# Products that nobody reads on TensorE, in a decoder of four layers: at the seams between stages and in front of waits inside them

## The reference

```python
x = _layernorm(x + _L0_attn_ref(x, L0_attn_W_in, ...), axis=-1)
x = _layernorm(x + _L0_xattn_ref(x, ctx_768, L0_xattn_Wq, ...), axis=-1)
x = _layernorm(x + _L0_ffn_ref(x, L0_ffn_gate_w, ...), axis=-1)
...
x = _layernorm(x + _L3_ffn_ref(x, L3_ffn_ln_scale, ...), axis=-1)
```

```python
# layer 1, feed-forward
logits = xf @ Wr                                  # 8 columns
top_vals, top_idx = jax.lax.top_k(logits, TOP_K)
...
h = _sq_relu(jnp.einsum('td,edf->tef', xf, W1))
# layer 2, feed-forward
d2 = x2 + p2[None, :] - 2.0 * (xf @ prototypes.T) # 32 columns
w = jax.nn.softmax(-jnp.sqrt(jnp.maximum(d2, 0.0)) / t, axis=1)
topw, topi = jax.lax.top_k(w, 2)
```

## Time and profile before

| what | value |
| --- | --- |
| timed runs | 3248.4, 3252.83 and 3253.66 us |
| median | 3252.83 us |
| span of the profiled execution, first to last instruction | 3262.6 us |
| a time of its own for the profiled execution, beside the span | none given |
| PE busy | 2508.7 us (77%), 15890 products |
| DVE, ACT, POOL busy | 57%, 45%, 31% |
| granted TensorE clock, mean of the span | 0.879 |
| DMA, mean | 53 GB/s |

### The profile page before, as it was taken

The page is one execution under the profiler, slowest core; times in us unless marked ns, Lnnn a source line. Parts: engine busy times, 40 slices in busy tenths (PEclk is TensorE's granted clock), DMA queues, the critical chain, the costliest instruction groups (busy, mean ns, idle before and its releaser), DMA issues. The chain is left out here.

```text
span 3262.6 us, 45065 instructions
## 1 busy us (share of the span) xinstructions
PE 2508.7 (77%) x15890; PEld 1399.0 (43%) x15890; DVE 1855.3 (57%) x5014; ACT 1480.5 (45%) x2984; POOL 996.1 (31%) x822
## 2 busy tenths in 40 slices
PE   6788885785667577888874669897776788859977
PEld 2323324564443233333352255564443333346666
DVE  6576655565645455555553558335432577656678
ACT  5334451453432156666641514224412355537876
POOL 1145561146347566666612300001101111101200
PEclk9889998897878789999986869997687799978989
DMA  3311101610444411111002210001000322114023
GB/s 112 94 43 42 42 2 36 229 54 19 125 154 101 108 47 46 35 41 46 17 15 67 34 39 1 10 4 30 14 1 33 74 28 28 16 48 123 1 78 104
DMA packets 186942, 174.52 MB, mean 53 GB/s; under 512 B 52777, under 2 KB 160042, under 8 KB 186462
## 3 DMA queue, kind: packets, MB, share of 16 engines
q1 hardware_dynamic: 172030, 153.84, 16.8%
q0 software_dynamic: 9408, 12.56, 2.5%
q10 hardware_dynamic: 5280, 5.24, 0.5%
HBM read 117.62 MB, written 57.40 MB: 54 GB/s over the span
## 5 line engine op out<-in xcount | busy, mean ns | idle before, releaser
L946 POOL TENSOR_TENSOR l1a_p_lo<-res,l1a_p_hi 128x1024 f16<-128x1024 f32 x192 | 311.9, 1643 | 177.2 <-ACT res L1187 177.2
L1196 ACT ACTIVATE l0a_probs<-ps 128x1024 f32<-128x1024 f32 (+1 forms) x192 | 145.5, 810 | 176.2 <-PE ps L1050 103.7
L1196 ACT ACTIVATE l3a_probs<-ps 128x1024 f32<-128x1024 f32 (+1 forms) x192 | 146.9, 809 | 143.3 <-PE ps L1050 116.2
L1186 ACT ACTIVATE l1a_p_hi<-ps 128x1024 f16<-128x1024 f32 x192 | 157.8, 822 | 110.9 <-PE ps L1050 82.8
L1047 PE MATMUL ps<-l1a_qs,l1a_ks 128*128 128x512 f16 (+3 forms) x768 | 167.7, 333 | 31.6 <-ACT res L1187 31.6
L1016 PE MATMUL ps<-l1a_ks,l1a_qs 128*128 128x512 f16 (+3 forms) x384 | 122.2, 347 | 78.7 <-DVE l1a_nmax L1221 33.0
L1218 DVE CUSTOM_DVE_ANT_0 l1a_masked<-ps,l1a_wide_mask 128x128 bf16<-128x128 f32 (+3 forms) x256 | 118.0, 490 | 103.1 <-PE ps L1016 100.9
L971 POOL TENSOR_TENSOR l0a_both<-l0a_probs 128x768 f32<-128x768 f32 (+2 forms) x96 | 154.7, 1633 | 46.3 <-PE ps L1088 46.0
L1187 ACT ACTIVATE res<-ps 128x1024 f32<-128x1024 f32 x192 | 158.1, 823 | 0.0
L1050 PE MATMUL ps<-mask_t,ident_b 128*128 128x128 bf16 x768 | 157.5, 225 | 0.0
L1218 DVE CUSTOM_DVE_ANT_0 l0a_masked<-ps,l0a_wide_mask 128x128 bf16<-128x128 f32 (+3 forms) x256 | 116.5, 489 | 68.0 <-PE ps L1016 67.3
(11 more groups left out here) (749 smaller groups left out, 6453.7 us busy)
## 6 DMA issues: line engine op xcount, KB each, us to landing
f_wf<-in_L_ffn_w_dram SPq DMA_DIRECT2D x16, 1024.0 KB
f_slots<-x0a_zeros SPq DMA_DIRECT2D x32, 256.0 KB, 3.4
f_xe<-f_slots SPq DMA_DIRECT2D x32, 256.0 KB, 3.0
f_ys<-f_y SPq DMA_DIRECT2D x32, 256.0 KB
l1a_qs<-l_q_h SPq DMA_DIRECT2D x64, 128.0 KB
d_wall<-in_L_ffn_W_dram SPq DMA_DIRECT2D x3, 2112.0 KB
l0a_qs<-l_q_h SPq DMA_DIRECT2D x32, 128.0 KB
l0a_ks<-l_k_h SPq DMA_DIRECT2D x16, 256.0 KB
```

The costliest lines, as they stand in the source:

```text
L946: pool.tensor_tensor(ph_lo[:, n % SLOTS, :, 0:w], probs[:, n % FULL, :, 0:w], ph_hi[:, n % SLOTS, :, 0:w], ALU.subtract).then_inc(s_["low_ ...
L1186: act.activation(ph_hi[:, n % SLOTS, :, 0:w], SB[n % 2][:, :, 0:w], ACT.Exp)
L1196: act.activation(probs[0:KR, n % SLOTS, 2 * pr:2 * pr + 2, 0:w], SB[x % 2][:, :, 0:w], ACT.Exp).then_inc(s_["exps"], 1)
```

## The change

A new function issues n products into a PSUM bank that the place does not use at that moment. Each multiplies the 128x128 16-bit identity with the identity repeated four times, 512 columns; nobody reads the result, and no semaphore is signalled by it. Calls of it are put at 112 places that issue 893 such products in the whole program. Where the place stands in front of a wait on data, a wait on the bank's last reader is moved ahead of it, or added.

```diff
+    def keep_busy(self, pe, bank, n):
+        for _ in range(n):
+            pe.matmul(bank, self.ident_b[:], self.ident_b[:, None, :].to_broadcast([P, 4, P]), start=True, stop=True)
...
 class Tail: __init__
+        self.busy = (0, 0)
 class Tail: tensor
+        after(pe, ph.s["xts_ready"], g)
+        if g == NG - 1:
+            ph.k.keep_busy(pe, self.tp[:, 0, :], self.busy[0])
         pe.wait_ge(ph.s["xn_ready"], g + 1)
-        after(pe, ph.s["xts_ready"], g)
         for c in range(DC):
...
         ins.then_inc(ph.s["xn_turned"], 1)
+        if g == NG - 1:
+            ph.k.keep_busy(pe, ph.k.ps[:, 2, :], self.busy[1])
 norm_program
-            pe.wait_ge(ph.s["n_xc_ready"], g + 1)
             if g >= NB:
                 pe.wait_ge(ph.s["n_ready"], g - NB + 1)
+            if within:
+                k.keep_busy(pe, TP[g % NB][:, 0, :], 9)
+            pe.wait_ge(ph.s["n_xc_ready"], g + 1)
 packed_attention, the row factor
                         pe.wait_ge(s_["maxed"], a - NSA + 1)
+                        if own_sums and plan.key_rows == P:
+                            k.keep_busy(pe, sa, 9)
                         pe.wait_ge(r_ld[s % KEEP], 32 * (s // KEEP + 1))
 packed_attention, scores
-                    if u.first and pr == 0:
-                        pe.wait_ge(m_ld[s % LEAD], 32 * (s // LEAD + 1))
...
+                    if plan.key_rows < P and n == 0 and pr == 0:
+                        k.keep_busy(pe, k.ps[:, 2, :], 18)
+                    if u.first and pr == 0:
+                        pe.wait_ge(m_ld[s % LEAD], 32 * (s // LEAD + 1))
 project_columns
+        tail.busy = (40 if pre else 20, 4)
+                k.keep_busy(pe, k.ps[:, 2, :], 16 if pre else 12)
                 pe.wait_ge(ph.s["w_ld"], n_ld)
 project_halves
+        tail.busy = (16, 4)
+                k.keep_busy(pe, k.ps[:, 2, :], 28)
 turn_out
+        tail.busy = (14, 4)
 project_out
+                tail.busy = (16, 4)
 l0_self_attention, for each batch b and c in range(EC)
+                            if b:
+                                pe.wait_ge(ph.s["v_ready"], b * TB)
+                            k.keep_busy(pe, PV[0], (0, 4, 4, 9)[c])
 project_in, busy=8
+            k.keep_busy(pe, k.ps[:, 0, :], busy)
 rotary_projection
+                if t % GT < 3:
+                    k.keep_busy(pe, k.ps[:, 5, :], 4)
             def columns(g):
+                if g:
+                    pe.wait_ge(s_["v_moved"], g)
+                k.keep_busy(pe, k.ps[:, 6, :], 11)
                 pe.wait_ge(s_["xn_ready"], g + 1)
...
                 ins.then_inc(s_["xn_turned"], 1)
+                k.keep_busy(pe, k.ps[:, 6, :], 8)
 l3_self_attention, stage l3e
+                    k.keep_busy(pe, k.ps[:, 0, :], 14)
 context, start and end
+                k.keep_busy(pe, bank[0], 20)
+                k.keep_busy(pe, k.ps[:, 4, :], 16)
 cross_operators, start and end
                 if columns is None:
+                    k.keep_busy(pe, bank[0], 16 if shared else 11)
                     turned_context(pe)
                 products(pe, done, NJ)
+                k.keep_busy(pe, k.ps[:, 6, :], 12)
 cross_rows, turn of batch a of tile t, x = NBT * t + a
-                    pe.wait_ge(s_["normed"], NH * t + needs[a])
                     if x >= 2:
                         pe.wait_ge(s_["lower"], x - 1)
+                    if x == 0:
+                        k.keep_busy(pe, TP[0], 14 if NH > 1 else 6)
+                    elif NH == 1:
+                        k.keep_busy(pe, TP[x % 2], 2)
+                    pe.wait_ge(s_["normed"], NH * t + needs[a])
 routed_experts, start
+                k.keep_busy(pe, k.ps[:, 0, :], 7)
 l1_feed_forward
+                k.keep_busy(pe, k.ps[:, 1, :], 4)
                 pe.wait_ge(s_["g_ld"], 16)
...
                 hidden(0)
+                k.keep_busy(pe, k.ps[:, 2, :], 24)
                 pe.wait_ge(s_["gates_ready"], 1)
...
+                k.keep_busy(pe, k.ps[:, 0, :], 18)
                 columns(NG - 1)
+                k.keep_busy(pe, k.ps[:, 0, :], 4)
 l2_feed_forward
                 def turn(t):
-                    pe.wait_ge(s_["weighted"], t + 1)
                     if t >= 2:
                         pe.wait_ge(s_["moved"], t - 1)
+                        k.keep_busy(pe, TP[t % 2], 4)
+                    pe.wait_ge(s_["weighted"], t + 1)
...
+                k.keep_busy(pe, k.ps[:, 4, :], 10)
                 pe.wait_ge(s_["p_ld"], 32)
...
                 lower(1)
+                k.keep_busy(pe, k.ps[:, 5, :], 16)
...
+                k.keep_busy(pe, k.ps[:, 0, :], 11)
                 columns(NG - 1, NT)
+                k.keep_busy(pe, k.ps[:, 0, :], 4)
```

More of the change, by code:

```diff
@@ L1824, in row_parts, with project_in @@
     return parts
-def project_in(k, ph, jobs, loads, split=False, early=None, apart=False):
+def project_in(k, ph, jobs, loads, split=False, early=None, apart=False, busy=8):
     nc = k.nc
```

## The result

The changed kernel took 3229.97 us at the median (3226.85 to 3238.05), the kernel before 3253.24 us; the ratio is 0.993, 95% interval [0.9913, 0.9947]. That is 23.3 us saved where 49.3 were forecast. The direction was right and the time lies inside the stated range, but the size is less than half.

What follows compares the result with a forecast made beforehand. PE was taken as busiest, its work after waits slowed by a low clock (24% of the span). Gains of 80.5 us less costs of 31.2 gave 49.3 us off the 3252.8 median: 3203 us, own range 3180 to 3222, outer 3160 to 3240.

Steps and rivals of the forecast that it cites:

- the sum inside stages: Forecast terms for the 537 products inside stages, neither at starts, last turns nor ends: 34.4 us saved.
- Items 1 and 2: Ten cold stage starts and the last turns of stages' outputs: products in the waits raise the clock, 17.5 and 5.4 us saved.
- Item 4: f2, the stage of prototypes: 4.0 us saved at its cold front, 11.5 in six later cold stretches.
- Item 3: Waits inside x1a, x0a, the expert stage's gate turn, l1p and x3c: cold PE work halved, 14.2 us saved.
- Item 5: x2a: 12 us gained in four cold stretches, less 6.5 for two products per tile without a wait; 5.5 saved.
- Item 6: l3a, nine products before each of 16 row-factor products: 11.7 us gained, 13.6 lost at steps without a wait; net -1.9.
- Item 7: Products ahead of the barriers after x0c, x2c and x3c delay the next stage: 8.0 us cost, 4.4 of it at x3c.
- Item 8: l0p: nine products twice where PE does not wait cost more than the clock returns, -0.6 us; l1p 0.
- The first rival: Less comes back inside stages because VectorE or ScalarE is next once PE is faster: 28.1 us saved, 3225; 15%.
- The rule weighed: Ramping penalty below 1% of a typical span would put the prize under 33 us; the prediction said the trace disagrees.

Runs made afterwards that it cites:

- e2: Changed kernel without the products at stage starts, last turns and stage ends (537 inside stages left); 0.997 of the kernel before, 3249.1 us.
- e1: Changed kernel without the products inside stages (356 at starts, last turns and ends left); 0.9941 of the kernel before, 3238.74 us.
- e8: e5 with 16 wide products mixed into f2's 32-column products and eight products, not four, starting f1; 0.9842 of the kernel before, 3204.11 us.
- e5: Changed kernel with products only where its trace shows a wait, as many as it holds (683 left); 0.9865 of the kernel before, 3212.95 us.
- e6: e5 with wide products mixed into f2's 32-column (16) and f1's 8-column products (24); 0.9859 of the kernel before, 3210.96 us.
- e9: e8 with 24 wide products also mixed into f1's 8-column products; 0.9837 of the kernel before, 3205.41 us.
- e4: The kernel before, unchanged, run again for a second trace; 0.9986 of the kernel before, span 3251.1 us.

## Why the prediction failed, step by step

The step that failed is the sum inside stages, above all items 4 and 3: 34.4 us were forecast there and e2 gave 6.8. It failed in two ways: gains were sized from cold stretches whose waits the products did not fill, and the costs of products behind a wait that ends last were not counted. The cost that stood in the sum for the ends of stages did not come either, and hid part of this.

- *Items 1 and 2, starts and last turns (22.9 forecast).* Right in the mechanism, somewhat large. From the mean of the four traces without wide products to that of the two with them, x1c shortened from 17.3 to 14.4 us, l3e from 10.0 to 8.0, l2p from 47.6 to 46.2 and x2c from 18.7 to 16.7, each within 0.3 us of half its cold start; x0c did not. In e1 these items and item 7 gave 17.2 us where 14.9 were forecast. That they agree is partly luck: the ends cost nothing in e1, so starts and turns alone gave 17.2 of 22.9 (the interval reaches to 26), and a cost of 8.0 that did not come made up for it.
- *Item 4, f2 (15.5).* Mis-sized most: 4.0 us, from a mean of 151.3 us in the four traces without wide products to 147.3. PE's own work at the low level fell from 49.5 us in the first trace to 27.9, halved 10.8; e8 leaves 6. As allowed for ("one of the waits may be too long for four products"), one was: it is the wait of 3.3 us of the third turn, in three groups. What the forecast lacked is that `moved`, put ahead of the four, is the wait that ends last in three other turns (3.4 us). Half of the front's 9.6 us was allowed; the ten products lifted the clock and the narrow ones let it fall, and 13.8 of the next 17.6 us ran at the low level. e5 undid the first two and f2 gave 10 us more. And the trace read was one with 153.2 us; a second of the same kernel has 148.3, so part of the prize stood in that execution alone.
- *Item 3 (14.2).* x3c: 4.1 us forecast, about 3 lost. The nine products stand behind a copy that ends within 0.3 us of the data behind them, so there was no wait left to fill. x3c is 68.2 us in e2, which has the nines and no products at the end, and 65.7 us in e1, which has those at the end and no nines. x1a and x0a: 4.0 and 2.4 forecast, 1.3 and, without the first trace, 0.5 us seen, which is inside their scatter. l1p, with the expert stage ahead of it, took 321.7 and 321.0 us, and 321.6 to 325.1 without the wide products: 1.5 us would fit. The gates and f1's front, with its start and last turn, gave 3.3 of 5.
- *Item 5, x2a (5.5).* 0.5 us, from a mean of 85.0 to 84.6. The clock came as forecast: own work at the low level fell from 39.4 us in the first trace to 16.2, halved 11.6 where 12 were taken. The cost of two products 0.43 us fifteen times, 6.5 us, was counted; so about 4 us more of the gain lay off the path or in the scatter. In e5, e6, e8 and e9, without the six products ahead of the first turn, x2a is 80 to 83 us, but in e2, with them, it is 81.6. What these five lack together is the twelve products at the end of x2c; no run takes that apart.
- *Item 6, l3a (-1.9).* The mechanism was right in both directions, and both sizes were near. The prediction counted seven steps with a wait and nine without; there are eight of each. Six steps without one take 18.3 us from row factor to row factor in the changed kernel and 16.4 in e5, which has no products there, and two more are 2.0 and 1.9 us longer. That is 15.3 us; with what other waits give back it is 11.4 us from the first row factor to the last (244.7 against 233.3), where 13.6 were forecast. On the other side 11.7 us of gain were forecast, and own work at the low level fell from 49.8 us in the first trace to 23.1, halved 13.4. The net is small beside the scatter: -1.9 was forecast, and the four lengths without wide products have a mean of 311.1 us, the two with them 315.5.
- *Item 7, the ends (-8.0).* Over-sized: 2.8 us at x3c in one trace and none in the other, nothing to be seen at x0c, x1c and x2c. What failed is the wait: the sum took VectorE's end at 2965.3 for what opens the barrier and added its 2.1 us whole. Of these, 1.1 us are SP's wait for its store, in which PE's products cost nothing; that wait ends 2.6 us behind PE's last own product at x2c, and 1.9 us behind it at x3c. "The same 0.8 us by which VectorE ends after PE" was the wrong slack.
- *Item 8, l0p (-0.6).* The nine products cost their 1.9 us twice, but the clock gave 1.7 back only once; the second time it fell ahead of them instead (twelve products in 4.18 us). l0p has 145.5 and 143.8 us against 141.8 to 143.3.

The first rival, less comes back inside stages, had the better number (3225) and the wrong reason: it put another engine in PE's place. e5 shows that PE was still next in f2 and l3a, since placing alone made them 10 and 11 us shorter. For x0a, x1a and x2a its reason stays possible; no run tells. The profiled execution's excess of 9.8 us over the median stood for the most part in stages that a second trace has shorter (x0a by 6.5 us, f2 by 4.9), and taking the saving off the median was right.

e8 recovers 1.6% of this kernel's time, by [0.9824, 0.9861]; the change itself recovers 0.7%. The rule weighed, that the penalty of ramping is below 1% of a typical kernel's span (the Trainium skill, TensorE: Matmul & The Clock Gate, Part 1, "What's actually happening"), does not hold for this kernel by e8; the change's 0.7% alone would have fitted it.

What stays open: how much of the 76 to 94 us of PE time lay off the path from the start, and how much a stage's luck with the clock hides; the scatter of x1a (101.6 to 107.5 us with the same products) is as large as most terms.

## What to carry to other kernels

A filler product costs its whole time wherever the wait that ends last stands ahead of it, be it the wait for its own bank; find for each place which of the two waits ends last, and how long it is, per step and not per loop, and put the filler between them in that number or leave it out. The starts of stages and their last turns are the safe places: here 356 of 893 products, with those at the ends, gave 17 us of 24. Ahead of a barrier, look for what opens it; here it was mostly SP's wait for a store, and products there cost nothing while they ended sooner, but no run shows that they gain anything. And read the low-clock stretches in at least two traces before they are added up: in f2 they differed by 5 us between two executions of one kernel.

## What the runs showed of the hardware that was not expected

- The same stretch of 88 mixed products, with PE busy throughout, ran for 20.4 us at a granted clock of 0.51 in e6 and for less than 12 us at 1.00 in e9. What differed was four wide products or eight ahead of it: in e6 the clock fell 0.6 us into the stretch and did not come back in it.
- 893 products with 8 columns, in waits or not, left the mean clock at 0.887, against 0.886 in e4 without them, and cost no time that could be measured (0.9975 and 0.9996).
- One kernel's stage can differ by 5 to 7 us between executions, and half the difference in own work at the low level comes to about as much: f2 148.3 and 153.2 us (39.0 and 49.5 us low), l3a 304.6 and 311.7 (36.4 and 49.3).
- At the four seams behind x0c, x1c, x2c and x3c the barrier of the kernel before opens on the landing of SP's last store: at x2c 2.6 us behind PE's last own product, at x3c 1.9 us.
